# Recurrent attention: a scan over four tokens a step instead of two, with the joining of the pairs shared between GpSimd and VectorE

## The reference, cut to what matters

```python
def step(state, inp):
    r_t, d_t, k_t, v_t, a_t, b_t = inp
    sa = jnp.einsum('bhij,bhj->bhi', state, a_t)
    state = state * d_t[:, :, None, :] + sa[..., None] * b_t[:, :, None, :] + v_t[..., None] * k_t[:, :, None, :]
    return (state, jnp.einsum('bhij,bhj->bhi', state, r_t))
```

## Time and profile before

| | us |
|---|---|
| median of 3 runs (lowest to highest) | 3829.98 (3829.01 to 3832.07) |
| the profiled execution, its own time | 3834.17 |
| its span in the profile | 3832.4 |
| the arrays, from the span's start to the scan's first ACT instruction | 281.0 |
| the scan, from the first step to the last | 292.3 to 580.2 |
| everything behind the block of the scan | about 3250 |

### The profile page before, as it was taken

One profiled execution on the slowest core, in us unless ns is written; L12 is line 12 of the kernel. 1 busy time (PEld: TensorE's weight loads), 2 busy tenths in 40 slices (PEclk: granted clock), 3 DMA queues, 4 the chain that ended last, 5 costly groups with the idle time before them and its releaser, 6 DMA issues. The chain is left out here.

```text
span 3832.4 us, 57780 instructions
## 1 busy us (share of the span) xinstructions
PE 2914.7 (76%) x17280; PEld 1926.9 (50%) x17281; DVE 2201.8 (57%) x5694; ACT 1916.6 (50%) x4554; POOL 1502.3 (39%) x1451
## 2 busy tenths in 40 slices
PE   5549995565972768999999968999649368597798
PEld 1116772343972435555555634555448324354576
DVE  7857883540134467766678845666412458685344
ACT  4446652421652517777878737777336346110232
POOL 0002220116034039877888823444253533364000
PEclk8869997876986859999999978999779779598799
DMA  3440002122661010000000004443458312000000
GB/s 62 73 83 1 11 6 78 44 88 76 168 186 44 27 51 19 18 14 18 18 18 14 17 19 122 123 122 114 134 152 233 89 57 83 2 0 1 24 0 22
DMA packets 198724, 232.54 MB, mean 61 GB/s; under 512 B 26481, under 2 KB 161378, under 8 KB 198114
## 3 DMA queue, kind: packets, MB, share of 16 engines
q1 hardware_dynamic: 183778, 206.70, 19.8%
q0 software_dynamic: 8192, 16.79, 1.4%
q10 hardware_dynamic: 6528, 6.29, 1.1%
HBM read 165.26 MB, written 40.36 MB: 54 GB/s over the span
## 5 line engine op out<-in xcount | busy, mean ns | idle before, releaser
L2961 POOL TENSOR_TENSOR local_size<-local_size,local_half_powers 128x8 f32<-128x8 f32 x128 | 257.5, 2011 | 19.1 <-issue 0.6
L2671 PE MATMUL bank<-local_wqkv,local_shifted 128*128 128x512 f32 x384 | 216.8, 649 | 21.9 <-DMA local_shifted<-normed_t 19.1
L1067 DVE TENSOR_TENSOR moe_outs<-bank,moe_record 128x128 f32<-128x128 f32 x160 | 46.2, 291 | 315.7 <-PE bank L763 292.1
L843 ACT ACTIVATE moe_hid<-bank,moe_record 128x128 f32<-128x128 f32 x640 | 182.9, 370 | 79.5 <-PE bank L750 75.4
L1581 POOL TENSOR_TENSOR ssm_decay<-ssm_decay,ssm_future 128x1024 f32<-128x1024 f32 x64 | 137.4, 2149 | 209.1 <-DMA ssm_decay<-ssm_sums_of 209.1
L883 POOL DMA_INDIRECT moe_found<-moe_sorted_outs,moe_slots x128 | 123.1, 962 | 240.8 <-DMA moe_sorted_outs<-moe_outs 168.1
L4039 POOL TENSOR_TENSOR rwkv_added<-rwkv_values_of,rwkv_rows_of 128x256 f32<-128x256 f32 x128 | 80.3, 628 | 284.7 <-PE bank L4014 203.7
L2852 ACT ACTIVATE local_probs<-bank,local_peak 128x128 f32<-128x128 f32 x512 | 184.5, 400 | 5.1 <-issue 2.9
L763 PE MATMUL bank<-moe_seconds,moe_hid 128*128 x1280 | 180.1, 286 | 3.8 <-ACT moe_hid L843 1.6
L750 PE MATMUL bank<-moe_rows_t,moe_record 128*128 128x128 f32 x1280 | 179.7, 286 | 0.0
L119 POOL TENSOR_TENSOR branch_norm_shifted<-branch_norm_moments,eps 128x4 f32<-128x4 f32 x48 | 9.6, 201 | 432.3 <-DVE branch_norm_moments L112 432.1
(11 more groups left out here) (584 smaller groups left out, 8341.5 us busy)
## 6 DMA issues: line engine op xcount, KB each, us to landing
moe_record<-in_moe_records_dram SPq DMA_DIRECT2D x160, 322.0 KB
ssm_decay<-ssm_sums_of SPq DMA_DIRECT2D x64, 768.0 KB, 5.0
mamba_decay<-mamba_sums_of SPq DMA_DIRECT2D x16, 768.0 KB
moe_sorted_rows<-moe_found SPq DMA_DIRECT2D x20, 512.0 KB, 6.4
moe_rows_in<-moe_sorted_rows SPq DMA_DIRECT2D x80, 128.0 KB
moe_sorted_outs<-moe_outs SPq DMA_DIRECT2D x80, 128.0 KB
local_across<-local_values SPq DMA_DIRECT2D x64, 128.0 KB, 2.3
rwkv_kept<-rwkv_keep SPq DMA_DIRECT2D x8, 768.0 KB, 15.0
```

The costliest lines, as they stand in the source:

```text
L843: last = act.activation(hid[:, k % 2, f, :], hbank[k % 2][:, f * UNIT:(f + 1) * UNIT], ACT.Gelu_apprx_tanh, bias=record[:, k, B1 + f:B1 + ...
L2671: pe.matmul(bank[:], shifted[:, at, t * P:(t + 1) * P], wqkv[:, of // 2 // PAIRS, part * INNER:(part + 1) * INNER], start=True, stop=True) ...
L2961: pool.tensor_tensor(part, part, half_powers[:], ALU.pow).then_inc(scaled, 1)
```

## The change

The scan takes four tokens a step: 64 steps, `CK = 4` steps per block of 16 tokens. In each step `recalled` has five parts instead of three, the reduction covers four of them, `removed` is two instructions of two tokens each, and `shown` covers four tokens. POOL multiplies v and k for four tokens and adds the four products in two more instructions, so that PE has one matmul for `added`, one for the decayed state and four for `removed`; it now runs two of the `turn_out` matmuls per step.

For that, pairs of tokens are joined into fours in the arrays stage, in a new routine `quad`. For each pair of sequences POOL makes four products of 512 columns (`dot`), one decay product of 128 columns, three decays in place, four `total` and four `add` instructions of 256 columns. PE sums them with four more matmuls of 512 columns, into banks 6 and 7, and DVE multiplies these banks in four instructions of 512 columns (`quad_first` at the end of the same pair, `quad_second` behind the next pair's `blend`). The DMAs of w and k move from ACT's queue to SP's, each behind POOL's new semaphores. ACT waits for `keep_ready` before it overwrites w.

```diff
-    STEPS = SEQ // 2
+    STEPS = SEQ // 4
...
+        decay_four = [isb(f"decay_four{s}", [P, HALF // 2]) for s in range(2)]
+        dots, totals = isb("dots", [P, 2, PN]), isb("totals", [P, 2, HALF])
...
             for i in range(PAIRS):
                 s = i % 2
+                sp.wait_ge(recall_ready, i + 1)
+                send(sp, "w", i, sent[s][1])
                 sp.wait_ge(rates_ready, i + 1)
-                send(sp, "d", i, decay_two[s])
+                send(sp, "d", i, decay_four[s])
                 send(sp, "b", i, sent[s][4])
+                sp.wait_ge(keys_ready, i + 1)
+                send(sp, "k", i, sent[s][2])
                 sp.wait_ge(recv_ready, i + 1)
                 send(sp, "r", i, sent[s][0])
                 sp.wait_ge(keep_ready, i + 1)
...
+            def quad(q, second):
+                pe.wait_ge(dots_ready, q * 2 + second + 1)
+                if not second:
+                    pe.wait_ge(crossed_used, q + 1)
+                for n, bank in enumerate((WITH_B, WITH_K)):
+                    pe.matmul(core.bank[bank][:], heads[:, 0, :], dots[:, n], start=True, stop=True).then_inc(dots_up, 1)
...
+                if has_last:
+                    quad(i - 1, 0)
                 if has_next:
                     attn.pe(pe, i + 1)
+                if has_last:
+                    quad(i - 1, 1)
...
+            quad(PAIRS - 1, 0)
+            quad(PAIRS - 1, 1)
...
+                if i >= 2:
+                    act.wait_ge(keep_ready, i - 1)
...
-                if i > 0:
-                    send_keys(i - 1)
...
-            def send_keys(q):
-                act.wait_ge(keys_ready, q + 1)
-                send(act, "w", q, sent[q % 2][1])
-                send(act, "k", q, sent[q % 2][2])
...
-            with pool.Fori(0, PAIRS) as i:
+            def powers(i):
                 pre.power_shifted(pool, i)
                 attn.pool(pool, i)
+            def dot(n, first, then):
+                return pool.tensor_tensor(crosswise(dots[:, n]), half_of(first, 0).unsqueeze(3).broadcast_to(CROSS),
+                                          half_of(then, 1).unsqueeze(2).broadcast_to(CROSS), ALU.mult)
+            def fade(rows, h, decay):
+                mine = half_of(rows, h)
+                return pool.tensor_tensor(mine, mine, pair_decay(decay, 1 - h).unsqueeze(2).broadcast_to(FOURS), ALU.mult)
+            def total(n, axis):
+                parts = crosswise(dots[:, n])
+                pool.tensor_tensor(by_two(totals[:, n]), *(parts[:, :, m, :] if axis == 0 else parts[:, :, :, m]
+                                                           for m in range(2)), ALU.add)
+            def add(rows, n):
+                return pool.tensor_tensor(rows, rows, by_two(totals[:, n]), ALU.add)
+            def quad(q):
+                s = q % 2
+                r, w, k, v, b = (rows[:] for rows in sent[s])
+                decay = decay_two[s][:]
+                pool.wait_ge(crossed_used, q + 1)
+                if q > 0:
+                    pool.wait_ge(dots_up, 4 * q)
+                dot(0, b, w)
+                dot(1, k, w).then_inc(dots_ready, 1)
+                if q >= 2:
+                    pool.wait_ge(landed["d"][s], 32 * (q // 2))
+                pool.tensor_tensor(decay_four[s][:], pair_decay(decay, 0), pair_decay(decay, 1), ALU.mult)
+                pool.drain()
+                pool.wait_ge(shown_joined, q + 1)
+                fade(w, 1, decay)
+                pool.wait_ge(parts_ready, 2 * q + 1)
+                total(0, 0)
+                total(1, 1)
+                pool.drain()
+                add(half_of(w, 1), 0).then_inc(recall_ready, 1)
+                dot(0, b, r)
+                dot(1, k, r).then_inc(dots_ready, 1)
+                pool.drain()
+                fade(r, 1, decay)
+                fade(b, 0, decay).then_inc(rates_ready, 1)
+                fade(k, 0, decay)
+                pool.drain()
+                add(half_of(k, 0), 1).then_inc(keys_ready, 1)
+                pool.drain()
+                pool.wait_ge(parts_ready, 2 * q + 2)
+                total(0, 0)
+                total(1, 0)
+                pool.drain()
+                add(half_of(r, 1), 0).then_inc(recv_ready, 1)
+                add(half_of(keep[s][:, 0, :], 1), 1).then_inc(keep_ready, 1)
+                pool.drain()
+            powers(0)
+            for i in range(PAIRS):
+                if i < PAIRS - 1:
+                    powers(i + 1)
+                if i > 0:
+                    quad(i - 1)
+            quad(PAIRS - 1)
...
-                    dve.wait_ge(landed["d"][s], 32 * (q // 2))
+                    dve.wait_ge(keys_ready, q - 1)
...
-                dve.tensor_tensor(even(b[:]), even(b[:]), odd(d[:]), ALU.mult).then_inc(rates_ready, 1)
+                dve.tensor_tensor(even(b[:]), even(b[:]), odd(d[:]), ALU.mult)
...
-                dve.sem_inc(keys_ready, 1)
...
-                dve.tensor_tensor(keep[s][:, 0, :], core.bank[WITH_K][:], v[:], ALU.mult)
+                dve.tensor_tensor(keep[s][:, 0, :], core.bank[WITH_K][:], v[:], ALU.mult).then_inc(crossed_used, 1)
...
-                dve.tensor_tensor(odd(r[:]), odd(r[:]), product[:, 0:HALF], ALU.add).then_inc(recv_ready, 1)
+                dve.tensor_tensor(odd(r[:]), odd(r[:]), product[:, 0:HALF], ALU.add).then_inc(shown_joined, 1)
...
-                                         ALU.add, ALU.mult).then_inc(keep_ready, 1)
+                                         ALU.add, ALU.mult)
+                dve.drain()
...
+            def parts_of(n, factor):
+                bank = core.bank[(WITH_B, WITH_K)[n]]
+                return dve.tensor_tensor(crosswise(dots[:, n]), crosswise(bank[:]), factor.broadcast_to(CROSS), ALU.mult)
+            def quad_first(q, s):
+                r, w, k, v, b = (rows[:] for rows in sent[s])
+                dve.wait_ge(dots_up, 4 * q + 2)
+                parts_of(0, half_of(w, 0).unsqueeze(3))
+                parts_of(1, half_of(b, 1).unsqueeze(2)).then_inc(parts_ready, 1)
+            def quad_second(q, s):
+                r, w, k, v, b = (rows[:] for rows in sent[s])
+                dve.wait_ge(dots_up, 4 * q + 4)
+                parts_of(0, half_of(w, 0).unsqueeze(3))
+                parts_of(1, half_of(v, 0).unsqueeze(3)).then_inc(parts_ready, 1)
                 dve.drain()
...
                 blend(i)
+                if i >= 2:
+                    quad_second(i - 2, s)
                 if i > 0:
...
                 if i > 0:
                     finish(i - 1, 1 - s)
+                    quad_first(i - 1, 1 - s)
...
+            quad_second(PAIRS - 2, 0)
             products(PAIRS - 1, 1)
             across(PAIRS - 1, 1)
             finish(PAIRS - 1, 1)
+            quad_first(PAIRS - 1, 1)
+            quad_second(PAIRS - 1, 1)
...
-    CK = 8
+    T = 4
+    STEPS = SEQ // T
+    CK = 4
...
-                    pe.matmul(bank, core.ident[:], added[:, s, 0, :], start=True, stop=False)
-                    pe.matmul(bank, core.ident[:], added[:, s, 1, :], start=False, stop=False)
+                    pe.matmul(bank, core.ident[:], added[:, s], start=True, stop=False)
+                    if has_last:
+                        turn_out(m - 1, 2 * k, 1 - slot)
                     pe.wait_ge(recalled_ready, c + 1)
-                    pe.matmul(bank, core.ident[:], recalled[:, s, 2, :], start=False, stop=False)
-                    pe.wait_ge(removed_ready, c * 2 + 1)
-                    pe.matmul(bank, core.ident[:], removed[:, s, 0, :], start=False, stop=False)
-                    pe.wait_ge(removed_ready, c * 2 + 2)
-                    pe.matmul(bank, core.ident[:], removed[:, s, 1, :], start=False, stop=True).then_inc(state_ready, 1)
+                    pe.matmul(bank, core.ident[:], recalled[:, s, T], start=False, stop=False)
+                    for t in range(T):
+                        if t % 2 == 0:
+                            pe.wait_ge(removed_ready, c * 2 + t // 2 + 1)
+                        last = pe.matmul(bank, core.ident[:], removed[:, s, t], start=False, stop=(t == T - 1))
+                    last.then_inc(state_ready, 1)
                     if has_last:
-                        turn_out(m - 1, k, 1 - slot)
+                        turn_out(m - 1, 2 * k + 1, 1 - slot)
...
+                pool.tensor_tensor(products[:].rearrange("p t (h i j) -> p (t h) i j", h=PH, j=HD), v.broadcast_to(shape),
+                                   key.broadcast_to(shape), ALU.mult)
+                pool.drain()
+                pool.tensor_tensor(halves[:], products[:, 0:2], products[:, 2:4], ALU.add)
+                pool.drain()
                 if not (isinstance(c, int) and c < 2):
                     pool.wait_ge(state_ready, c)
-                pool.tensor_tensor(out.rearrange("p (a i) j -> p a i j", i=HD),
-                                   v.rearrange("p (a i) o -> p a i o", i=HD).broadcast_to(shape),
```

(26 more changed lines are left out.)

74 lines of the change are left out of this document (43 added, 31 removed).

## The result

The changed kernel took 3875.4 us (median of 4) beside 3831.0 for the kernel before on the same chip: ratio 1.0118, interval 1.0097 to 1.0139, so 44 us slower. Its profiled execution took 3873.6, span 3871.6, which is 39.2 above the span of before. The forecast was 3901.

What follows compares the result with a forecast made beforehand. DVE was taken to bound the arrays stage, DVE's chain and PE's last two matmuls the scan step. Arrays +103 and scan -32 gave +71: 3905 us profiled, 3901 as median; range 3785 to 3940.

Steps and rivals of the forecast that it cites:

- Rival 1: Arrays and scan: POOL's and DVE's instructions pass each other without collisions; net -39 us, 3790; chance 0.18.
- Scan, own work: Scan: a step without collisions takes 3.37 us; 64 steps are 216 against 288, 72 us less.
- Scan, collisions: Scan: POOL's products and halves delay removed, step 4.0 us; 64 steps are 256 against 288, 32 us less.
- Arrays, VectorE's own part: Arrays, per pair without collisions: quad_first 1.3, waiting for PE 0.6, quad_second 1.3; 3.2 us.
- Arrays, collisions: Arrays: POOL's work seen by DVE costs 11.0 of 13.9 us a pair; six pairs make 83 us.
- rival 2: Arrays and scan: half the collisions, POOL's instructions falling into drains and PSUM-fed stretches; net +17 us, 3847; chance 0.17.
- GpSimd's work: Arrays: POOL's quad is four dots of 1.26, one 128-column and eleven 256-column instructions (0.63); 12.3 us per pair.
- End of the stage: Arrays, last pairs: pair 6 costs 9 us more plus 0.6 behind it, pair 7 15.4 more.
- Issue gain: Arrays: DMAs of w and k leave ACT's queue, so idle time before the blends comes back; 5 us, range 0 to 10.
- Rival 3: Scan: halves misses both removed, step 3.37 us, arrays as forecast; 3861; chance 0.12.
- rival 4: Arrays and scan: POOL 1.43 times slower on short strides, arrays +142, scan +14; 3985 us; chance 0.06.

Runs made afterwards that it cites:

- thin_pool: Changed kernel with every GpSimd quad instruction in the arrays stage cut to one group of columns; pair 34.0 us against 40.0, first recalled at 324.9 against 372.2.
- scan_early: Changed kernel with GpSimd's products waiting for both removed halves of the step before, and ScalarE staging keys and values first; step 3.432 us, ratio 1.0045.

## Why the prediction was right, and what was mis-sized

Direction and mechanism held: VectorE's instructions with two operands in SBUF got longer beside GpSimd, and the kernel got slower. Rival 1 (no collisions) fell to thin_pool, where the collisions were taken away and the pair was 34.0. The size was 44 us instead of 71. The steps of the sum:

- **Scan, own work**: 3.37 a step forecast, 3.35 in a clean step, 3.43 as the mean of scan_early. Right.
- **Scan, collisions**: 4.0 forecast, 3.875 measured, so the scan gave back 40 us instead of 32. I had put GpSimd's instructions at one fixed place in the step. They wander: a removed pair took from 0.76 to 2.16, on average 0.5 us a step over a clean one (I took 0.63). And products was 1.07, not twice 0.63.
- **Arrays, VectorE's own part** (quad_first, quad_second and the wait for sums, with no collisions): 3.2 a pair in rival 1, 3.4 measured as thin_pool less before. The wait in it was 1.65, not 0.6; that the total fits is partly luck, as a part of the waits of before went at the same time.
- **Arrays, collisions: the term that was mis-sized.** The forecast said "So I cost every POOL instruction that meets a two-SBUF instruction of DVE at its own length", and had 11.0 us a pair, of GpSimd's 12.3, seen by VectorE. VectorE's instructions got 7.5 longer, of GpSimd's 14.0; the pair got 6.0 longer by it, the rest being hidden in waits for TensorE. By place: key and finish 2.3 instead of 3.0 (0.94 for L3938, 0.90 for L3940, 0.48 for L3955), turn_rows 0.6 instead of 2.1 (L128 took 1.72 instead of 1.11; the sum fell on a read of PSUM and the first dot on the blend's idle 1.06), blend 2.75 instead of 3.4, products 1.8 instead of 2.5. What I had overrated is how much of GpSimd's work meets a VectorE instruction that minds. That was rival 2's thought, and the truth lay between it and the forecast.
- **GpSimd's work**: here the forecast was too low. Its dots took the 1.26 that I had taken, but a decay of 256 columns took 0.74 instead of 0.63. The quad also has one instruction more than I had counted: four decays in place (w, r, b and k), not three, so twelve of 256 columns and not eleven. That error worked against the one above.
- **End of the stage**: the two terms made 25. From the eighth blend to the first recalled it is 99.8 instead of 70.0; 3.5 of these 29.8 lie ahead of T0 of pair 6 and belong to pair 5, which leaves 26. L3901 (before: L3805) stood at T0 + 21.0 (forecast 20.2), kept was issued at + 20.7 (forecast 20.2). Right. The 3.5 us that I took for TensorE's two sums there stood on no row; the trace after has 3.54 at 332.48 and 3.66 at 308.34, at a granted clock of 0.55 and 0.53, near the lower of its two levels.
- **Issue gain**: idle time before the blends 15.3 instead of 19.0: 3.7 back, 5 forecast.
- **Rival 3** was ruled out by the steps (3.875), rival 4 by dots of 1.26: on runs of two elements 256 columns cost 0.74 for 0.63, not 1.43 times as much.

On the profiled execution the forecast of 3905 was 31 us too high: 23 from the arrays, nearly all of it the collisions of the pairs, and 8 from the scan.

## What to carry to other kernels

Work moved from VectorE to GpSimd is not free while VectorE reads two operands from SBUF: here 14 us of GpSimd's work per pair made VectorE's instructions 7.5 us longer and the pair 6 us, and the pair was no shorter than with VectorE doing the work itself. Before judging such a change, count which VectorE instructions lie beside it, and put one operand of those in a free PSUM bank: two such edits, with the rows that GpSimd needs staged first, turned 1.2% slower into 0.4% faster with the same work on GpSimd. A wait that keeps two engines apart works only if nothing else sets the start: look at the step in which it fails.

## What was not expected of the hardware

- VectorE's multiply by a per-partition scalar (TENSOR_SCALAR, 512 columns) reads a single SBUF tensor and still took 1.27 us instead of 0.49 beside GpSimd. Written to PSUM it took 0.75 and was not held up. The Trainium skill fits both (VectorE: DVE Perf Modes, Why PSUM operands drop a tier): the fast mode takes both SBUF read ports and is lost with any PSUM operand. The trace agrees, with 0.49 in SBUF and 0.75 to PSUM, though here it is the output that is in PSUM and not what is read.
- GpSimd is slowed too: mean 1.42 us for the second dot of a quad (k with w), which took 1.27 alone, and 1.07 instead of 0.74 for a decay of 256 columns beside the mixes (L3792). Which of the two ends first depends on the place.
- In the scan, GpSimd's multiply took 1.07 us for 512 columns, the dots of the arrays 1.26 for the same number. Both read two broadcast operands; the innermost run is eight elements in the scan and two in the dots. Whether that makes the difference was not tried.
